# The opening of a perceiver kernel: latents normed once, weights in pieces, the plan moved, and products of zeros on TensorE

## What is computed

```python
def layer_norm(x, g, b):
    return (x - mean) * rsqrt(var + 1e-05) * g + b
x = x + xattn(ctx_1024, _layernorm(x), mask, g1, b1, g2, b2, Wq, Wkv, Wout)
# inside xattn, with 16 heads of 64:
xn, ln_lat = layer_norm(context, g1, b1), layer_norm(latents, g2, b2)
q = ln_lat @ Wq
k, v = split(concatenate([xn, ln_lat]) @ Wkv)
weight = softmax(where(mask or latent, (q * s) @ (k * s).T, -max))   # s = 64 ** -0.25
out = (weight @ v) @ Wout
x = x + attn(_layernorm(x), Qw, Kw, Vw)      # causal, one head
x = x + ffn(_layernorm(x), ...)              # two layers of local attention and feed-forward
```

## Time and profile before

| | us |
|---|---|
| median of 3 runs | 1072.71 |
| lowest, highest | 1072.39, 1073.54 |
| span of the profiled execution | 1071.0 |

### The profile page before, as it was taken

One profiled execution on the slowest core, in us unless ns is written; L12 is line 12 of the kernel. 1 busy time (PEld: TensorE's weight loads), 2 busy tenths in 40 slices (PEclk: granted clock), 3 DMA queues, 4 the chain that ended last, 5 costly groups with the idle time before them and its releaser, 6 DMA issues. The chain is left out here.

```text
span 1071.0 us, 25673 instructions
## 1 busy us (share of the span) xinstructions
PE 1017.7 (95%) x8678; PEld 944.8 (88%) x8679; DVE 822.1 (77%) x3031; ACT 663.1 (62%) x1542; POOL 205.3 (19%) x265
## 2 busy tenths in 40 slices
PE   3899999999999999999999999988999999999997
PEld 3789999999999999999999998976879898989897
DVE  5897877777777777777777777578888889889753
ACT  4466565665565665565665566475676777667653
POOL 0111111111111111111111111350006203164213
PEclk9999999999999999999999998998999999999999
DMA  6000000000000000000000100420001000010000
GB/s 202 23 3 12 11 1 0 11 4 10 13 2 0 11 3 11 13 2 0 11 3 11 34 2 1 155 47 1 2 6 55 2 2 21 21 60 2 2 21 21
DMA packets 29073, 21.71 MB, mean 20 GB/s; under 512 B 13269, under 2 KB 26537, under 8 KB 28969
## 3 DMA queue, kind: packets, MB, share of 16 engines
q1 hardware_dynamic: 27985, 20.21, 6.3%
q10 hardware_dynamic: 984, 0.13, 0.1%
HBM read 19.23 MB, written 1.05 MB: 19 GB/s over the span
## 5 line engine op out<-in xcount | busy, mean ns | idle before, releaser
L295 PEld LDWEIGHTS pv_ps<-v,pt 128*128 128x128 f32 x1792 | 216.0, 193 | 8.8 <-issue 2.4
L295 PE MATMUL pv_ps<-v,pt 128*128 128x65 f32 x1792 | 216.4, 273 | 2.7 <-DVE o L820 1.4
L798 DVE CUSTOM_DVE_ANT_0 s_sb<-s_ps,pen,mstate 128x256 f32<-128x256 f32 (+1 forms) x512 | 199.9, 447 | 13.3 <-issue 10.4
L493 ACT ACTIVATE probs<-s_sb,mbias 128x256 f32<-128x256 f32 (+1 forms) x512 | 203.1, 469 | 0.0
L660 POOL TENSOR_TENSOR o<-o,alpha 128x260 f32<-128x260 f32 x128 | 86.2, 673 | 572.6 <-ACT alpha L487 572.6
L502 ACT ACTIVATE pt<-turn 128x512 f32<-128x512 f32 x128 | 76.2, 595 | 121.3 <-PE turn L282 107.4
L282 PE MATMUL turn<-ident,probs 128*128 128x128 f32 x896 | 124.3, 279 | 4.1 <-DVE ql L776 3.2
L282 PEld LDWEIGHTS turn<-ident,probs 128*128 128x128 f32 x896 | 99.1, 145 | 14.2 <-DVE ql L776 3.4
L820 DVE TENSOR_TENSOR o<-o,pv_ps 128x260 f32<-128x260 f32 x128 | 54.0, 422 | 46.9 <-PE pv_ps L295 36.1
L271 PE MATMUL s_ps<-kh,qh 64*128 64x256 f32 (+1 forms) x512 | 79.4, 306 | 4.2 <-DVE kl L770 1.8
L770 DVE TENSOR_TENSOR kl<-proj,kh 128x512 fp32r<-128x512 f32 (+1 forms) x63 | 41.2, 655 | 50.0 <-ACT kh L480 49.7
(11 more groups left out here) (420 smaller groups left out, 2743.9 us busy)
## 6 DMA issues: line engine op xcount, KB each, us to landing
raw<-in_ctx SPq DMA_DIRECT2D x24, 128.0 KB, 2.1
f_wqkv_raw<-in_L_ffn_wqkv SPq DMA_DIRECT2D x6, 512.0 KB, 5.3
wkv_raw<-in_L_xattn_Wkv SPq DMA_DIRECT2D x2, 1024.0 KB, 8.4
f_w_raw<-in_L_ffn_w SPq DMA_DIRECT2D x8, 256.0 KB, 5.0
f_w_raw<-in_L_ffn_w SPq DMA_DIRECT2D x2, 640.0 KB
wq_raw<-in_L_xattn_Wq SPq DMA_DIRECT2D x1, 1024.0 KB, 8.8
wout_raw<-in_L_xattn_Wout SPq DMA_DIRECT2D x1, 1024.0 KB, 10.2
f_wo_raw<-in_L_ffn_wo SPq DMA_DIRECT2D x2, 512.0 KB, 4.5
```

The costliest lines, as they stand in the source:

```text
L295: last = pe.matmul(t.pv_ps[:, u, :], t.pt[g % 2][:, u, kt, :], t.v[:, kt, h, :], start=(kt == 0), stop=(kt == kts - 1))
L493: last = act.activation(t.probs[g % 2][:, u, 0:kts * P], t.s_sb[g % 2][:, u, 0:kts * P], ACT.Exp, bias=t.mbias[:, at:at + 1], scale=0.125)
L798: last = dve.tensor_tensor_reduce(out=t.s_sb[g % 2][:, u, 0:width], in0=t.s_ps[g % 2][:, u, 0:width], in1=t.pen[:, 0:width], scale=1.0, sc ...
```

## The change

- The latents are normed once. ScalarE's logarithm takes (1 + eps) times the variance plus eps squared, which gives the factor of both norms together; VectorE reads `x` itself. `latent_moments`, `latents_normed` and `first_deviations` are gone, for batch 0 in the opening and for the six other tiles in step 0.
- Wq and the keys' half of Wkv come in six transfers: columns 0 to 255 of each, 256 to 511 of each, 512 to 1023 of each; ScalarE splits a piece when its columns are there. The value half is issued once the second pair has landed.
- Gains, offsets and the table of first keys are loaded as rows of 128 numbers. TensorE turns them (one transpose and two small products), VectorE copies them out of PSUM.
- `plan`, `plan_sums` and the low parts of weight pieces 6 and 7 go behind the first and second maxima in step 0; the statistics of step 1's tokens go from j = 0 to j = 2, their norm from j = 2 to j = 3. ScalarE makes the high parts of pieces 6 to 9 after the high parts of keys 1.
- TensorE multiplies zeros (from `o`, which GpSimd has zeroed): four pairs of 64x256 products first of all, five pairs after the first transposes. A pair's two products write the lower and the upper 64 partitions of a score bank.

The core of the diff:

```diff
-    def load_norm(eng, which, told):
+    def load_norm(eng, which):
 
         for part, name in enumerate("gb"):
-            with nc.allow_non_contiguous_dma("a vector of the width onto the partitions"):
-                eng.dma_start(t.norm[:, which, part * KC:(part + 1) * KC],
-                              args[f"L0_xattn_{name}{which + 1}"].rearrange("(k p) -> p k", p=P)).then_inc(s[told], 16)
+            row = 2 * KC * which + KC * part
+            eng.dma_start(t.norm_rows[row:row + KC, :], args[f"L0_xattn_{name}{which + 1}"].rearrange("(k p) -> k p", p=P)
+                          ).then_inc(s["ident_loaded"], 16)
...
-            load_norm(sp, 1, "gain_loaded")
-            sp.dma_start(t.wq_raw[:], args["L0_xattn_Wq"].rearrange("(k p) n -> p k n", p=P)).then_inc(s["wq_loaded"], 16)
-            sp.dma_start(t.wkv_raw[:, :, key_cols], wkv[:, :, key_cols]).then_inc(s["wk_loaded"], 16)
-            sp.wait_ge(s["wk_loaded"], 16)
+            wq = args["L0_xattn_Wq"].rearrange("(k p) n -> p k n", p=P)
+            for q_told, k_told, cols in (("q_loaded", "k_loaded", slice(0, 256)), ("second_w_loaded", "second_w_loaded", slice(256, 512)),
+                                         ("third_w_loaded", "third_w_loaded", slice(512, H * DH))):
+                sp.dma_start(t.wq_raw[:, :, cols], wq[:, :, cols]).then_inc(s[q_told], 16)
+                sp.dma_start(t.wkv_raw[:, :, cols], wkv[:, :, cols]).then_inc(s[k_told], 16)
+            sp.wait_ge(s["second_w_loaded"], 32)
             sp.dma_start(t.wkv_raw[:, :, value_cols], wkv[:, :, value_cols]).then_inc(s["wv_loaded"], 16)
...
                     now = at_step(m, kind, prev, j - 3)
+                    if prev is None and j == 3:
+                        pe.wait_ge(s["plan_rows"], 1)
                     if now:
...
-            pe.wait_ge(s["ident_loaded"], 16)
+            def multiply_zeros(pairs):
+
+                for _ in range(pairs):
+                    for rows in (slice(0, DH), slice(DH, P)):
+                        pe.matmul(t.s_ps[1][rows, 0, :], t.o[:, 0, 0:DH], t.o[:, 1:5, 0:DH], start=True, stop=True)
+
+            pe.wait_ge(s["state_zero"], 1)
+            multiply_zeros(4)
+            pe.wait_ge(s["ident_loaded"], 80)
+            pe.transpose(t.turn[1][:, 0:4 * KC], t.norm_rows[:], t.ident[0:4 * KC, 0:4 * KC]).then_inc(s["norm_turned"], 1)
+            pe.wait_ge(s["keys_loaded"], 32)
+            pe.wait_ge(s["state_set"], 1)
+            pe.matmul(t.s_ps[0][:, 0, 0:P], t.ones_row[:], t.key_line[:], start=True, stop=True)
+            pe.matmul(t.s_ps[0][:, 2, 0:1], t.key_line[:], t.ones_row[:, 0:1], start=True, stop=True).then_inc(s["norm_turned"], 1)
             turn_tokens(0)
+            multiply_zeros(5)
             pe.wait_ge(s["x_ready"], 1)
             pe.wait_ge(s["w_lo"], 1)
             query(0, 0, True)
+            pe.wait_ge(s["w_lo"], 2)
+            project_keys(0, KB)
             pe.wait_ge(s["flags_ready"], 2)
             pe.matmul(t.pv_ps[:, 0, 0:1], t.below[:].rearrange("p b c -> p (b c)"), t.listed[:, NCH:NCH + 1], start=True, stop=True
                       ).then_inc(s["flags_ranked"], 1)
-            pe.wait_ge(s["w_lo"], 2)
-            project_keys(0, KB)
+            pe.wait_ge(s["w_lo"], 3)
+            query(0, 1, True)
             pe.wait_ge(s["keys_spread"], 1)
             pe.matmul(t.pv_ps[0:B, 1, 0:NCH + 1], t.row_of[:], t.listed[:], start=True, stop=True).then_inc(s["keys_listed"], 1)
-            pe.wait_ge(s["w_lo"], 3)
-            query(0, 1, True)
             pe.wait_ge(s["w_lo"], 4)
             project_keys(1, KB, key_bank(0, 1))
-            pe.wait_ge(s["plan_rows"], 1)
...
-            def deviations(m):
+            def deviations(m, latents):
                 act.wait_ge(s["var"], m + 1)
-                act.activation(t.std[:], t.mv[:, :, 1], ACT.Ln, bias=t.eps[:]).then_inc(s["std"], 1)
+                if latents:
+                    act.activation(t.std[:], t.mv[:, :, 1], ACT.Ln, bias=t.eps_squared[:], scale=1.0 + EPS).then_inc(s["std"], 1)
+                else:
+                    act.activation(t.std[:], t.mv[:, :, 1], ACT.Ln, bias=t.eps[:]).then_inc(s["std"], 1)
                 act.wait_ge(s["std"], m + 1)
                 act.activation(t.rstd[:], t.std[:], ACT.Exp, scale=-0.5).then_inc(s["rstd_done"], 1)
...
-                            if not final:
-                                deviations(m + 1)
+                            if prev is not None and not final:
+                                deviations(m + 1, kind == "half")
                         elif j == 2 and kts == 2:
                             store_values(m, 1, 1)
+                            if prev is None:
+                                deviations(m + 1, False)
...
-                            first_deviations(slice(QT, TILES), 2)
...
-            key_of = args["first_key"].rearrange("b (c o) -> (b c) o", o=1)
...
 
             act.dma_start(t.ident[:], args["ident"]).then_inc(s["ident_loaded"], 16)
-            with nc.allow_non_contiguous_dma("a number for each partition"):
-                act.dma_start(t.key_col[:], key_of).then_inc(s["keys_loaded"], 16)
-            act.dma_start(t.key_row[:], args["first_key"].rearrange("(o b) c -> o (b c)", o=1).partition_broadcast(P).rearrange("p o n -> p (o n)")
-                          ).then_inc(s["keys_loaded"], 16)
-            act.dma_start(t.iota[:], args["iota"]).then_inc(s["norm_loaded"], 16)
-            load_norm(act, 0, "norm_loaded")
-            first_deviations(slice(0, QT), 1)
-            deviations(0)
-            act.wait_ge(s["wq_loaded"], 16)
+            for which in (1, 0):
+                load_norm(act, which)
+            act.dma_start(t.key_line[:], key_line).then_inc(s["keys_loaded"], 16)
+            act.dma_start(t.iota[:], args["iota"]).then_inc(s["keys_loaded"], 16)
+            deviations(0, True)
+            act.wait_ge(s["q_loaded"], 16)
             weights_hi(range(0, 1))
-            act.wait_ge(s["wk_loaded"], 16)
-            weights_hi(range(1, 4))
+            act.wait_ge(s["k_loaded"], 16)
+            weights_hi(range(1, 2))
             tokens_hi(0)
+            act.wait_ge(s["second_w_loaded"], 32)
+            weights_hi(range(2, 4))
+            act.wait_ge(s["third_w_loaded"], 32)
             weights_hi(range(4, 6))
             query_hi(0, 0, True)
+            keys_hi(0, 0, KB)
+            query_hi(0, 1, True)
+            keys_hi(0, 1, KB)
             act.wait_ge(s["wv_loaded"], 16)
-            weights_hi(range(6, 7))
-            keys_hi(0, 0, KB)
-            weights_hi(range(7, 9))
-            query_hi(0, 1, True)
-            weights_hi(range(9, 10))
-            keys_hi(0, 1, KB)
+            weights_hi(range(6, 10))
...
-            def latent_moments(tiles, value):
-                for k in tiles:
...
-                    last = dve.bn_aggr(t.x_mv[:, k, :], t.x_stats[:, k, :])
...
-            def latents_normed(tiles, value):
-                dve.wait_ge(s["latents_step"], 5 * value - 1)
-                for k in tiles:
-                    last = dve.tensor_scalar(t.raw[:, 1 + k // QT, k % QT, :], t.x[:, k, :], t.x_mv[:, k, 0:1], t.x_rstd[:, k:k + 1],
...
-                    if j == 0:
+                    if prev is None and j == 0:
+                        plan()
+                        weights_lo(range(6, 8))
+                    elif prev is None and j == 1:
+                        query_lo(0, 2, True)
+                        plan_sums()
+                        query_lo(0, 3, True)
+                        weights_lo(range(8, 9))
+                    elif prev is None and j == 3:
+                        weights_lo(range(9, 10))
+                    elif prev is None and j in (5, 7):
+                        weights_lo(range(10, 12) if j == 5 else range(12, 14))
+                    if j == (2 if prev is None else 0):
                         if kind != "half":
                             dve.wait_ge(s["raw_loaded"], 32 * loads)
                             dve.memset(t.tick[:, 2:3], 0.0)
-                        statistics(m + 1, slot)
+                        statistics(m + 1, batch)
                         variances(m + 1)
-                    elif j == 2:
-                        normalised(m + 1, slot)
+                    elif j == (3 if prev is None else 2):
+                        normalised(m + 1, batch)
                     elif j == 5:
                         tokens_lo(m + 1)
                     elif j == 7:
                         penalties(b, kind, i, loads)
-                    if prev is None and j == 1:
-                        query_lo(0, 2, True)
-                        query_lo(0, 3, True)
-                        weights_lo(range(8, 9))
-                    elif prev is None and j == 2:
-                        weights_lo(range(9, 10))
+                    if prev is None and j == 6:
                         dve.wait_ge(s["rest_loaded"], 32)
```

(31 more changed lines are left out.)

45 lines of the change are left out of this document (19 added, 26 removed).

## The result

The changed kernel took 1068.95 us in the median (1068.75 to 1071.28, 5 runs) against 1072.71 for the kernel before on the same chip: ratio 0.9966, 95% interval 0.9954 to 0.9979. It is faster by 3.8 us, a third of a percent and clear of the spread of its runs, and half of the 7.5 that I had forecast. The profiled execution took 1066.9 us, 4.1 less than that of before.

What follows compares the result with a forecast made beforehand. TensorE, busy 95% of the span, bounds the kernel; its opening waits, 20.9 us, are what can be won. Transposes 7.15 us earlier plus 0.5 behind them, less 0.15 for handovers, give 7.5: 1065.2 us median, range 1062.5 to 1069.8.

Steps and rivals of the forecast that it cites:

- One norm: VectorE's opening: the pass that wrote raw writes z itself, done at 6.7 us, 2.4 us earlier.
- Weights in pieces: Weight loads in the opening: first piece at 6 us, second at 7, third pair at 10.0; hidden up to about 8.
- Zeros: TensorE's opening: paired halves overlap, four pairs take 4.0 us to 6.6; five more cover 8.4 to 10.8 us.
- that end, 13.2 us: Five pairs of zeros behind the latents' transposes: they end at 13.2 us at the lower clock, 10.8 at the higher.
- Its own sign of being wrong: TensorE's opening: the prediction is wrong if the first projection waits for its own zeros.
- The first projection: TensorE's first product of the tokens by weights: starts at 10.8 us instead of 17.0.
- The first maxima: VectorE's first maxima after four projections: start at 18.5 us instead of 28.27.
- To the second step's transposes: First maxima to step 1's transposes, set by VectorE's chain: 22.3 us instead of 19.7, transposes at 40.8 instead of 47.95.
- The fourth case: Plan behind the first maxima as a new wait: that stretch 25 us instead of 22.3, 1068.0 us in all; chance 12%.
- The second sign of being wrong: Prediction wrong if the 9.8 us gain at the first maxima shrinks under 5 us at the second step's transposes.
- Behind it: After the second step's transposes: the six tiles' norm at 65.11 us goes, 0.5 us of TensorE's waits saved.
- Carried through to the end as a shift: No TensorE idle from 48 to 64 us, so time won before the transposes at 47.95 us lasts to the end.

Runs made afterwards that it cites:

- Norm_alone: Changed kernel without the zeros and the six weight transfers, with the plan ahead of the first maxima: 1067.08 us, ratio 0.9930.
- after_again: The changed kernel run again unedited, for a second trace: 1066.63 us, ratio 0.9952.
- after_third: The changed kernel run unedited for the third time: 1068.05 us, ratio 0.9945.
- spare_only: Changed kernel with an unused 18-column tile declared, later tiles 72 bytes further, and no memset added: 1064.89 us, ratio 0.9906.
- memsets_only: Changed kernel with 18 memsets at VectorE's start into columns of the tile for z, no new tile: 1068.07 us, ratio 0.9936.
- after_shift: Changed kernel with a new 18-column tile and 18 memsets into it at VectorE's start: 1064.43 us, ratio 0.9908.
- both_shift: Changed kernel with two pairs of zeros behind the transposes, plan ahead of the first maxima, new 18-column tile and 18 memsets: 1064.35 us, ratio 0.9898.

## Why the prediction was right and wrong

- **One norm** was right: z started 1.64 us behind x's statistics, 2.4 earlier than with two. Norm_alone shows that norm and row loads together bring the most.
- **Weights in pieces**: the first landed as forecast. Where x was early, ScalarE began Wq's first columns at 5.7 and 5.9 us, forecast 6; in the first trace it was itself held by the late norm until 7.25. The last pair, forecast for 10.0, was there at 11.6 us in after_again and at 12.6 in after_third, where the high part of query 0 stood behind it; the sum had nothing for that. The step missed that their gain and that of the removed small loads are one gain: either part alone takes away the wait for Wq, and pieces on top bring nothing that the medians show.
- **Zeros**: the halves overlap. Sixteen records took 3.29 to 3.7 us (forecast 4.0); one after the other they would have taken 7.0 by the price of a record in the sum. What the Trainium skill says ("TensorEngine Tiling (Array Packing)", Key Properties), that tiles work independently, the traces bear out. The five pairs took 2.4 us as forecast where the clock stayed high, 4.07 and 4.5 where it fell. The forecast named that end, 13.2 us, and kept it out of the sum. Its own sign of being wrong, a first projection that waits for its own zeros, was there in the first trace, by 1.3 us, and not in the other two.
- **The first projection**, forecast 10.8: 12.75 in the first trace, 10.70 and 9.98 in the others. **The first maxima**, forecast 18.5: 20.84, 18.79, 19.75. After_again is where the sum put it. After_third was 0.8 us early and then took 1.7 us longer to the maxima than the other two, behind the late last pair of pieces. The first has x 1.4 us and the zeros 1.3 us late, of which 1.95 reached the projection.
- **To the second step's transposes**, forecast 22.3: 22.93, 22.98, 22.92. The chain was the one told, with VectorE waiting 1.2 us for keys 2, 1.2 for query 3 and 0.5 for the chunk, which landed as told 6.2 us behind the plan. 0.6 us too little. The fourth case put 25 us on the plan's wait; that didn't happen, though the clock fell there in each. The second sign of being wrong, under 5 us of gain left at these transposes, was there in the first trace (7.4 us at the maxima, 4.2 here), but because the opening was late and not because of the plan; the others had 6.2 and 5.3.
- **Behind it** I took 0.5 us; from the transposes to the step at 84 us the lead grew by 1.8 in two traces, and by 0.3 in the third, whose clock fell at 40 to 48 us.
- **"Carried through to the end as a shift"** is the step that failed. By it the lead of 84 us is that of the end. It lost 1.9, 2.0 and 1.9 us: 0.3 in the loop, 0.7 at one instruction of VectorE, about 1.0 at TensorE's gap. The 0.7 goes by the place of VectorE's instructions, as spare_only and memsets_only show. The 0.3 is put down to the place of the tiles by the pace of the products (0.120 against 0.118 us); no run undid that shift of the change. The cause of the gap stays open. I looked from 48 to 64 us for idle time and priced what the edit does to the work, and put at nothing that it moves the addresses of tiles and the places of instructions in every later stage.

For the profiled execution the sum reads: 7.65 forecast, -1.95 at the first projection, -0.4 to the maxima, -0.6 to the transposes, +1.3 behind it, -1.9 in the tail, 4.1 us. In after_again the first two terms are +0.1 and -0.4, in after_third +0.8 and -2.1; the tail is in all three. The three medians of the unedited kernel, 3.8, 6.7 and 6.2 us under before, show that the first was also at the low end; by them the forecast was too high by 0.8 to 3.7 us, and the tail explains 2.

The best versions are after_shift and both_shift, 1064.4 us, 9.8 us under before, against 6.2 for the unedited change beside after_shift. Both the expected and an unlooked-for gain are in them. The second is luck with an address and fragile: any tile declared ahead of `xt` may take it away.
